# Two attentions in a hybrid model: first pair's rows and last pair's sums placed by TensorE, three query blocks split beside the first maxima

## The reference

```
qkv = (x @ qkv_w.T + qkv_b).reshape(b, n, 3, 16, 8)          # first attention; n = 2048
scores = einsum('bnhd,bmhd->bhnm', q, k) / sqrt(8)
out = einsum('bhnm,bmhd->bnhd', softmax(scores), v).reshape(b, n, 128)
x = x + out @ out_w.T + out_b
```

## Time and profile before

| what | value |
|---|---|
| median of three runs | 3134.39 us |
| the profiled execution: its own time | 3127.79 us |
| its span, from the first to the last instruction | 3126.6 us |
| first maxima of the first attention | 36.89 us |
| last maxima of it end, its last addition to x ends | 629.02 us, 674.96 us |
| first maxima of the second attention | 1130.79 us |
| last addition to x of it ends | 1769.50 us |

### The profile page before, as it was taken

How to read it: one execution, slowest core, us unless ns; L and a number is a source line. 1 busy time by engine, 2 the same in 40 slices (tenths; PEclk the granted TensorE clock), 3 DMA queues, 4 the chain that set the end, 5 groups by cost and what they waited for, 6 DMA issues and landing times. The chain is left out here.

```text
span 3126.6 us, 57936 instructions
## 1 busy us (share of the span) xinstructions
PE 2814.4 (90%) x23088; PEld 1295.3 (41%) x23088; DVE 2495.0 (80%) x3276; ACT 2041.2 (65%) x3866; POOL 843.3 (27%) x978
## 2 busy tenths in 40 slices
PE   5999999978999969999999899999787798678788
PEld 1222222236666622222222366666332354356655
DVE  8999999955666679999999556666899856799544
ACT  4999999955555439999999555554766423645121
POOL 0100000012333301000000123333487571299510
PEclk6999999988999969999999889999999898888989
DMA  2000000000000010000000000000000000000000
GB/s 99 5 16 18 20 20 17 6 7 1 1 2 1 2 61 5 16 18 20 20 17 6 12 1 1 2 1 1 26 0 1 10 1 1 0 1 1 1 1 14
DMA packets 30216, 35.34 MB, mean 11 GB/s; under 512 B 13623, under 2 KB 24058, under 8 KB 29690
## 3 DMA queue, kind: packets, MB, share of 16 engines
q1 hardware_dynamic: 29754, 31.57, 3.5%
q10 hardware_dynamic: 192, 0.07, 0.0%
HBM read 19.16 MB, written 7.34 MB: 8 GB/s over the span
## 5 line engine op out<-in xcount | busy, mean ns | idle before, releaser
L420 DVE TENSOR_REDUCE max_parts<-banks 128x2 f32<-128x1024 f32 x1024 | 1169.0, 1218 | 18.8 <-PE banks L308 18.4
L510 ACT ACTIVATE probs<-banks 128x512 f32<-128x512 f32 x2048 | 1082.6, 599 | 73.9 <-PE banks L315 56.7
L308 PE MATMUL banks<-k_parts,q_parts 48*128 48x512 bf16 x2048 | 621.5, 396 | 48.4 <-DMA k_parts<-k_scratch 24.1
L315 PE MATMUL banks<-q_parts,k_parts 51*128 51x512 bf16 x2048 | 655.1, 386 | 6.6
L333 PE MATMUL banks<-probs,v_heads 128*9 128x256 f32 x8192 | 637.4, 382 | 7.5 <-ACT pv_copy L521 0.3
L315 PEld LDWEIGHTS banks<-q_parts,k_parts 51*128 51x128 bf16 x2048 | 148.0, 94 | 482.5 <-ACT probs L510 417.3
L550 POOL CAST neg_max_parts<-neg_max 128x8 bf16<-128x8 f32 x64 | 12.9, 201 | 1151.7 <-DVE neg_max L425 1151.7
L333 PEld LDWEIGHTS banks<-probs,v_heads 128*9 128x9 f32 x8192 | 123.8, 88 | 379.0 <-issue 340.4
L1495 POOL TENSOR_TENSOR state_times_c<-state,c_row 128x1024 f32<-128x1024 f32 x63 | 148.1, 2357 | 88.6 <-ACT c_row L1810 54.0
L1688 DVE TENSOR_TENSOR_SCAN state<-banks,state_carry,state 128x512 f32<-128x512 f32 x128 | 157.3, 1271 | 6.4 <-ACT banks L1805 4.3
L308 PEld LDWEIGHTS banks<-k_parts,q_parts 48*128 48x128 bf16 x2048 | 126.4, 94 | 79.2 <-DVE max_parts L420 50.0
(11 more groups left out here) (473 smaller groups left out, 5029.0 us busy)
## 6 DMA issues: line engine op xcount, KB each, us to landing
outT_half<-pv_copy SPq DMA_DIRECT2D x252, 16.0 KB
prob_sums<-pv_copy SPq DMA_DIRECT2D x252, 2.0 KB
q_scratch<-qk_parts SPq DMA_DIRECT2D x8, 384.0 KB, 3.9
k_scratch<-qk_parts SPq DMA_DIRECT2D x8, 384.0 KB, 2.5
k_parts<-k_scratch SPq DMA_DIRECT2D x32, 96.0 KB
q_parts<-q_scratch SPq DMA_DIRECT2D x28, 96.0 KB
k_parts<-k_scratch SPq DMA_DIRECT2D x32, 64.0 KB
q_parts<-neg_max_rows SPq DMA_DIRECT2D x128, 3.0 KB
```

What stands on the lines that cost most here:

```text
L308: nc.tensor.matmul(Mb[m % 2][:, blk(x)], Q[p % 2][half_of(x, ROWS), tile(t)], K[p % 2][half_of(x, ROWS), blk(b)], start=True, stop=True).t ...
L315: nc.tensor.matmul(bank("exp", n, x)[:, :], K[p % 2][half_of(x, ROWS + PARTS), tile(t)], Q[p % 2][half_of(x, ROWS + PARTS), blk(j)], start ...
L420: nc.vector.tensor_reduce(mxp[s % 2][:, :, u // NB, u % NB], Mb[m % 2].rearrange("p (x k) -> p x k", x=2), AX.X, ALU.max).then_inc(*maxed. ...
L510: nc.scalar.activation(PT[:, n % RING, x, :], bank("exp", n, x)[:, :], ACT.Exp, scale=float(HD) ** -0.5).then_inc(*exped.inc())
```

## The change

1. **First pair's rows.** For units 0 to 4 (q0, k0 to k3) the rows of pair 0 in `Q[0]` and `K[0]` are not fetched by DMA. TensorE multiplies the three parts by 0/1 matrices (`choose`, 3 bf16 matmuls of 512 columns for a unit), and ScalarE copies the result (`keep_chosen`), for the keys with a bias that makes the ones rows. `fill_keys(0)` goes.
2. **Units 5 to 7 (q1 to q3) later.** They are projected at m = 1, 2, 3; the subtraction that VectorE did is done by TensorE into the bank (`subtract`, at m = 4 to 6 and 8 to 10, one bf16 matmul each), and ScalarE cuts all three parts (`cut_from_bank`). Values are projected at m = 7, 14, 15, 16, the output bias at m = 18.
3. **DMAs.** The other query columns of pair 0 are still written to DRAM and read back; they are needed from m = 16 on.
4. **Columns.** VectorE's work for the columns is cut in three, behind the reductions of m = 2, 20 and 22 of the first attention.
5. **End.** The halves are added by TensorE: `start_sums(j, c)` has four float32 matmuls of 256 columns, `finish_sums(j, c)` two, which take the last pair directly from ScalarE's copy. The DMAs of the last four stages, GpSimd's additions and VectorE's addition of the sums go. `final_at` is 490, 497, 504, 515 (it was 490, 498, 506, 521).

The core of the diff ("..." marks what is left out):

```diff
+LATE_UNIT = 5
+BESIDE_AT = (2, 20, 22)
...
-        final_at = lambda j: max(STAGE * (STAGES - NB + j) + 25, UNITS_ALL - AHEAD + 3 + 8 * j)
+        final_at = lambda j: max(evacuate_at(STAGES - NB + j) + 1, UNITS_ALL - AHEAD + 3 + 7 * j)
+        start_at = lambda j: final_at(j) - (1 if j < NB - 1 else 5)
+        unit_bank = lambda n: g.ps[n % 4] if n < LATE_UNIT else g.ps[n]
+        choice_bank = lambda i: g.ps[4 + i % 4]
...
+                if n < LATE_UNIT:
+                    pe.wait_ge(rested, n - 3)
+                else:
+                    pe.wait_ge(chosen_copied, LATE_UNIT)
+                nc.tensor.matmul(unit_bank(n)[:, :], (w["wqT"], w["wkT"])[which], g.xnT[:, blk(b)], start=True, stop=True).then_inc(*projected.inc())
+
+            def choose(i):
+                pe.wait_ge(low, i + 1)
+                pe.wait_ge(chosen_copied, i - 3)
+                for a in range(PARTS):
+                    k = nc.tensor.matmul(choice_bank(i)[:, :], choice[:, which, a, :], part[:, i, a, :], start=(a == 0), stop=(a == PARTS - 1))
+                k.then_inc(*chosen.inc())
+
+            def subtract(n, a):
+                pe.wait_ge((high, mid)[a], n + 1)
+                nc.tensor.matmul(unit_bank(n)[:, :], minus[:, :], part[:, n, a, :], start=False, stop=True, skip_group_check=True).then_inc(*subtracted.inc())
...
-                pe.wait_ge(load_k[p % 2], 6 * (p // 2 + 1))
-                if s == 0:
-                    pe.wait_ge(q_first, 6)
+                if p == 0:
+                    pe.wait_ge(chosen_copied, b + 2)
                 else:
+                    pe.wait_ge(load_k[p % 2], 6 * ((p + 1) // 2))
+                if s > 0:
...
-            def spread_sums(j, c):
+            def start_sums(j, c):
                 pe.wait_ge(maxed, UNITS_ALL)
                 pe.wait_ge(sums_inverted, 2 * (j - 1) + c + 1)
-                pe.wait_ge(sums_added, j + 1)
-                nc.tensor.matmul(g.ps[c][:, 0:256], heads_up[:, :, :].rearrange("p h d -> p (h d)"), sums[:, 0, half_blk(j, c)],
-                                 start=True, stop=True).then_inc(*sums_spread.inc())
+                pe.wait_ge(x_added, 2 * (j - 1) + c + 1)
+                pe.wait_ge(gathered[j % 2], gathered_of(STAGES - 2 * NB + j + 2))
+                for k in range(2):
+                    nc.tensor.matmul(g.ps[c][:, 0:256], heads_up[:, :, :].rearrange("p h d -> p (h d)"), sums[:, k, half_blk(j, c)], start=(k == 0), stop=False)
+                for k in range(2):
+                    nc.tensor.matmul(g.ps[2 + c][:, 0:256], g.ident[:, :], oT[k][:, half_blk(j, c)], start=(k == 0), stop=False)
+
+            def finish_sums(j, c):
+                s, cols = STAGES - NB + j, slice(256 * c, 256 * c + 256)
+                pe.wait_ge(ends_made, 2)
+                pe.wait_ge(evacuated, s + 1)
+                nc.tensor.matmul(g.ps[c][:, 0:256], last_sums[:, :], osb[s % 2][:, cols], start=False, stop=True).then_inc(*sums_spread.inc())
+                nc.tensor.matmul(g.ps[2 + c][:, 0:256], last_outs[:, :], osb[s % 2][:, cols], start=False, stop=True).then_inc(*outs_spread.inc())
...
-            for n in range(2, len(units)):
+            for n in range(2, LATE_UNIT):
                 project_unit(n)
-                if n >= 4:
-                    project_values(n - 4)
-            pe.wait_ge(rested, len(units))
+            for i in range(LATE_UNIT):
+                choose(i)
+            pe.wait_ge(rested, LATE_UNIT)
...
-                if m == 8:
+                if 1 <= m <= 3:
+                    project_unit(LATE_UNIT - 1 + m)
+                if 4 <= m <= 6:
+                    subtract(LATE_UNIT - 4 + m, 0)
+                if 8 <= m <= 10:
+                    subtract(LATE_UNIT - 8 + m, 1)
+                for b in range(NB):
+                    if m == (7, 14, 15, 16)[b]:
+                        project_values(b)
+                if m == 18:
...
+                        if n == start_at(j) + c:
+                            start_sums(j, c)
                         if n == final_at(j) + c:
-                            spread_sums(j, c)
-                        if n == final_at(j) + 4 + 2 * c:
+                            finish_sums(j, c)
+                        if n == final_at(j) + 3 + c:
...
+                    if beside and m in BESIDE_AT:
+                        beside.on_dve(BESIDE_AT.index(m))
...
+            def cut_from_bank(n, a):
+                act.wait_ge(subtracted, n - LATE_UNIT + 1 + (len(units) - LATE_UNIT) * (a - 1))
+                nc.scalar.activation(part[:, n, a, :], unit_bank(n)[:, :], ACT.Identity, bias=(w["bq"], w["bk"])[which]).then_inc(*(mid, low)[a - 1].inc())
+
+            def keep_chosen(i):
+                act.wait_ge(chosen, i + 1)
+                if which:
+                    act.wait_ge(ones_made, 1)
+                    nc.scalar.activation(K[0][:, blk(b)], choice_bank(i)[:, :], ACT.Identity, bias=ones_at[:, :]).then_inc(*chosen_copied.inc())
+                else:
+                    nc.scalar.copy(Q[0][:, blk(b)], choice_bank(i)[:, :]).then_inc(*chosen_copied.inc())
...
-            for n in range(2, len(units)):
+            for n in range(2, LATE_UNIT):
                 cut_high(n)
                 cut_mid(n - 1)
-            cut_mid(len(units) - 1)
+                if n > 2:
+                    keep_chosen(n - 3)
+            cut_mid(LATE_UNIT - 1)
+            for i in range(LATE_UNIT - 3, LATE_UNIT):
+                keep_chosen(i)
+            for n in range(LATE_UNIT, len(units)):
+                cut_high(n)
+            cut_from_bank(LATE_UNIT, 1)
+            keep_values(0)
+            for n in range(LATE_UNIT + 1, len(units)):
+                cut_from_bank(n, 1)
+            for n in range(LATE_UNIT, len(units)):
+                cut_from_bank(n, 2)
             fill_keys(1)
-            for b in range(NB):
+            for b in range(1, NB):
                 keep_values(b)
             if beside:
...
-            for n in range(1 + NB):
+            for n in range(len(units)):
                 write(n)
-            sp.wait_ge(q_first_written, 1)
-            load_queries(q_first, 0, blk(0))
+            sp.wait_ge(chosen_copied, 1)
+            sp.wait_ge(q_written, NB - 1)
+            load_queries(load_q[0], 0, slice(512, N))
             sp.wait_ge(cleared, 1)
             sp.wait_ge(k_written, NB)
-            load_keys(load_k[0], 0)
-            for n in range(1 + NB, len(units)):
-                write(n)
-            sp.wait_ge(q_written, NB - 1)
-            load_queries(load_q[0], 0, slice(512, N))
-            sp.wait_ge(cleared, 2)
             load_keys(load_k[1], 1)
+            sp.wait_ge(q_first_written, 1)
             load_queries(load_q[1], 1, slice(0, N))
+            sp.wait_ge(ends_zeroed, 3)
             for s in range(STAGES):
                 send_negmax(s)
-                if s > 1:
+                if 1 < s < STAGES - NB + 2:
```

More of the change, by code:

```diff
@@ L408, in on_dve @@
             norm.apply(3)
-            for n in range(1, len(units)):
+            for n in range(1, LATE_UNIT):
                 split_rest(n)
                 split_low(n - 1)
-            split_low(len(units) - 1)
-            if beside:
-                beside.on_dve()
+            split_low(LATE_UNIT - 1)
             def reduce(m):
@@ L456, in on_dve @@
                             normalise(j, c)
-                        if n == final_at(j) + 5 + 2 * c:
+                        if n == final_at(j) + 4 + c:
                             add_x(j, c)
@@ L463, in cut_high @@
                 act.wait_ge(projected, n + 1)
-                nc.scalar.activation(part[:, n, 0, :], g.ps[n % 4][:, :], ACT.Identity, bias=(w["bq"], w["bk"])[which]).then_inc(*high.inc())
+                nc.scalar.activation(part[:, n, 0, :], unit_bank(n)[:, :], ACT.Identity, bias=(w["bq"], w["bk"])[which]).then_inc(*high.inc())
             def cut_mid(n):
@@ L485, in on_act @@
             norm.deviation(0)
-            fill_keys(0)
             norm.deviation(1)
@@ L567, in on_pool @@
                     add_bias(s - 1)
-            pool.wait_ge(max_split, 4 * STAGES)
-            for j in range(NB):
-                pool.wait_ge(gathered[j % 2], 8 * ((STAGES - NB + j) // 2 + 1))
-                nc.gpsimd.tensor_tensor(oT[0][:, blk(j)], oT[0][:, blk(j)], oT[1][:, blk(j)], ALU.add).then_inc(*halves_added.inc())
         def on_sp():
```

130 lines of the change are left out of this document (78 added, 52 removed).

## The result

The changed kernel takes 3149.70 us, the median of five runs (3149.36 to 3155.26), against 3131.98 us of the kernel before in five runs (3126.18 to 3135.00). The ratio is 1.0062, with an interval of 1.0050 to 1.0075 (the two medians alone give 1.0057): slower, by more than the 0.2% that can be told from no change. The forecast was 3148.0.

A forecast was written before the change was run, and what follows sets the result against it. VectorE's maxima bound the long middle, TensorE the end; terms of +10.8 and +2.8 us in the two attentions gave +13.6, so 3148.0 on the median of 3134.4, range 3133 to 3158.

The forecast's parts named there:

- the forecast's A: Whole kernel: TensorE's additions at full price, some stall at m = 16; 3148, own range 3141 to 3155; chance 0.55.
- Rival C: End of each attention: TensorE's added products are hidden, so faster, 3116 at no price; chance 0.13.
- rival B: At m = 16: no stall, the queries' DMA trip fits in 4.5 us; 3138, no measurable change; chance 0.17.
- First maxima: Start of each attention: rows placed by TensorE bring the first maxima 12.9 and 12.6 us earlier.
- Stall at m = 16: First stage: queries' DMA trip of 9.5 us against 4.5 left, +5.0 us in each attention (3.9 to 12.2).
- estimate of 8.4: Queries' DMA trip at m = 16, lower bound: a lone write of 2.5 plus 5.9 us for loads, stall 3.9.
- rival (D): First steps: TensorE at 1.2 GHz, some 2.5 us for each attention; 3153, or 3158 with a longer trip; chance 0.15.
- Columns and bias: VectorE's columns between reductions +5.7 us, first attention alone; bias behind the stall +3.1 in the first, +0.5 in the second.
- The end: Last maxima to ScalarE's last copy: TensorE's inserted products cost +16.0 us in each attention (13 to 17.8).
- my own 16.5: End of each attention: insertions cost 22.3 us against 5.8 before, 16.5 more; the rows' spacing gave 15.5, 16.0 was taken.
- Behind the last copy: From ScalarE's last copy to the last addition: one product replaces DMAs, addition and spread, -6.1 us in each attention.
- GpSimd beside VectorE: Start, 17 to 25 us: GpSimd's clearing could double four VectorE splits, 1 to 3 us for each attention, counted within rival (D).

The follow-up runs named there:

- old_end: Changed kernel with its end taken back (halves added by VectorE and GpSimd, last four stages gathered by DMA): 3129.50 us, 0.9983 of the kernel before.
- halves_pool: Changed kernel with half of the end's early products; GpSimd and VectorE add the gathered pairs' halves instead: 3140.43 us, 1.0013 of the kernel before.
- columns_late: Changed kernel with VectorE's and ScalarE's column work moved out from between the reductions, into waits: 3145.08 us.
- mixed_end: Changed kernel with the old end for j = 0 to 2; only j = 3 takes the last pair from ScalarE's copy: 3123.97 us, 0.9967 of the kernel before.
- q1_columns_mixed: Changed kernel with three edits: the end of mixed_end, queries of block 1 placed by TensorE, columns moved as in columns_late: 3116.57 us.
- scores_twice: Changed kernel with every score product of m = 0 to 24 issued twice into the same bank: 3154.86 us.

## Why the prediction was right, step by step

The total was right (3149.70 for 3148.0), and the mechanism is the forecast's A: the end's products are paid for, and the starts gain what the waits then take. Rival C is excluded by old_end and halves_pool, rival B by the 4.85 and 2.21 us of waiting TensorE. But the attentions grew by 22.6 us in the profiled executions where the sum had 13.6, so the sum was 9.0 too small. The forecast then went from the median, 6.6 above before's profiled execution, while after's profiled execution lies at its median. The two nearly cancel, so the hit within 1.7 us is in good part luck. The terms:

- **First maxima**: -12.4 and -13.6 for -12.9 and -12.6. Right; the chain of copies and cuts came out within a us.
- **Stall at m = 16**: the wait is there, mis-sized on both sides. The trip took 12.1 us in the first attention (ScalarE's last cut ends at 39.55, the product starts at 51.69) and 10.3 in the second (1146.77 to 1157.06), not 9.5. The window was not 4.5 but 7.3 and 8.1 us, since the blocks of values at m = 14 and 15 stand on TensorE ahead of that product, the later one for 1.75 and 2.08 us. Split at the first load's issue (44.42 below), the writes took 4.9 and 3.5 us where I had 3.6, the loads 7.3 and 6.8 where I had 5.9. The 2.5 us for a write came from the keys' row; the queries' own row in the same view of the kernel before, the last one below, has 3.9. The Trainium skill (DMA: Bandwidth & Descriptors, Anatomy of one DMA) gives its fit, about 2.0 us plus the bytes over 436 GB/s, for DMAs that GpSimd issues; these are issued by SyncE. Carried over to them, it gave the estimate of 8.4, and both trips took longer.

```profile
38.86 0.69 ACT L518 ACTIVATE qk_parts<-banks,mixer_weights 128x512 bf16<-128x512 f32 x1 [0.33 <-PE banks L309]
...
44.42 0.86 SPq L671 DMA_DIRECT2D q_parts<-q_scratch  x1
...
q_scratch<-qk_parts SPq DMA_DIRECT2D x4, 384.0 KB, 3.9
```

- **TensorE at 1.2 GHz in the first stage**: the step that was missing. I had the clock as a rival (D) for the projections; those ran at 2.4 GHz, and it was the values, moved from the wait ahead of the maxima to between them, that met 1.2 GHz: 1.01 + 1.01 us in the first attention, 1.01 in the second, all at nothing in the sum, and a gap of 1.32 behind m = 16 in both, for which it had 0.5. My argument against D also failed: before, the clock fell only behind more than 2 us of full rest; here it fell at about 33 us, and TensorE's longest rest in the 9 us before was 1.35.
- **Columns and bias**: 5.7 + 2.6 forecast as their own price in the first attention, 8.5 measured by columns_late. The total is right, in part by luck: 5.1 for VectorE's work and 2.35 for ScalarE's, and the gap of 1.01 from the clock, counted above already, makes up the rest.
- **The end**: +18.9 and +18.6 for +16.0, above my upper bound of 17.8 as well. The term that was mis-sized is `start_sums`: 2.12 us instead of 1.91, since the 0.20 of the switch comes once for each of the two groups, not once for the insertion: 1.7 us in each attention. The rest is the 0.5 that I took off my own 16.5 towards the rows' spacing, and small slack.
- **Behind the last copy**: -5.9 and -5.6 for -6.1. Right.
- **GpSimd beside VectorE**: no price here. The low part's split keeps the 0.68 us of the earlier trace rows while GpSimd clears a tile, as these rows of the first attention show. The Trainium skill (GPSIMD Engine Reference, Specifications) names contention for VectorE instructions with two SBUF inputs, which this one has. With a memset on GpSimd's side, which reads nothing, the trace does not show it; beside a GpSimd instruction that reads, no run tried it.

```profile
18.60 3.50 POOL L625 MEMSET prob_sums<- 16x4096 f32 x1
...
20.27 0.68 DVE L448 TENSOR_TENSOR qk_parts<-qk_rest,qk_parts 128x512 bf16<-128x512 f32 x1
```

## What to carry to other kernels

A small stage that hides in a wait is not free once the wait goes: list what lay under it (here the values, the columns and the issues on SyncE) and price each where it lands, at the clock that the engine has there. Where one engine is the bound, take the new route only for the piece that stands behind everything else: the last block's halves on TensorE save 5.7 and 5.2 us behind the last copy for some 2.5 ahead of it (mixed_end), the other three blocks only cost. And after each wait removed, read the next one in the trace before adding up prices.

## What was not expected of the hardware

- The stretch from the second attention's end to the end of the program, whose code no experiment touches, took 1355.1 to 1357.1 us in the profiled executions of five kernels (before and after among them) and 1361.7 to 1363.3 in the other seven. In one of the latter, q1_columns_mixed, the selective scan took 292.1 us at a granted clock of 0.92, against 288 at 0.95 in the changed kernel:

```profile
2176.50:2468.60 292.10, 236.08 (x580) 90.26 (x580) 259.93 (x269) 195.35 (x363) 189.95 (x90) 0.92 0.02 7
```

```profile
2215.00:2503.00 288.00, 230.36 (x580) 88.39 (x580) 259.87 (x272) 195.29 (x363) 189.93 (x90) 0.95 0.02 7
```

  That is 4 of the 6 us. They come and go between executions of one kernel too (3149.4 to 3149.7 and 3155.1 to 3155.3 us among the changed kernel's five). What sets them stays open.
- A float32 product of 256 columns costs 0.62 us where the group before it is another (halves_pool), and about 0.43 where it follows one of its own group (1.06 for two in the changed kernel), both at 2.4 GHz.
- The same four products of the values take 1.16 us at 2.4 GHz and 2.07 at 1.2. In the first attention the values of m = 7 are slow in the changed kernel and fast both in columns_late, where TensorE rests less ahead of them, and in scores_twice, where it has more work.
